# First state-space layer: kernel K directly behind the projection; expert block 0 in another order of steps

## What is computed

```
# state-space part, four layers i
z = layernorm_channels(h); K = 2 * Re(sum_n C[h,n] * exp(dtA[h,n] * l))
y = causal_convolution(z, K) + z * D_skip;  out = W @ gelu(y) + b
h = h + out[:H] * sigmoid(out[H:])
# experts: 12 experts, three routers (top 3 of 12, softmax over the three), 64-wide addresses
x_addr = x @ P_w.T;  dw1, dw2, dw3 = route(x_addr @ U1.T), route(x_addr @ U2.T), route(x_addr @ U3.T)
h = sum_e dw1[:, e] * (x @ W1[e].T);  h = gelu(h)
y = sum_e dw2[:, e] * (h @ W2[e].T) + dw3 @ b2
```

## Time and profile before

| | |
|---|---|
| median of 3 runs | 1193.77 us |
| profiled execution | 1192.28 us, of which the span on the core 1190.2 us |
| PE busy | 1002.9 us (84% of the span) |
| DVE, ACT, POOL busy | 761.6, 530.1, 446.3 us |
| chain that ended last, by engine | PE 57%, DVE 17%, POOL 13%, ACT 6%, issue 4% |
| mean granted TensorE clock | 0.907 of full speed |

### The profile page before, as it was taken

One profiled execution on the slowest core, in us unless ns is written; L12 is line 12 of the kernel. 1 busy time (PEld: TensorE's weight loads), 2 busy tenths in 40 slices (PEclk: granted clock), 3 DMA queues, 4 the chain that ended last, 5 costly groups with the idle time before them and its releaser, 6 DMA issues.

```text
span 1190.2 us, 19912 instructions
## 1 busy us (share of the span) xinstructions
PE 1002.9 (84%) x8002; PEld 668.9 (56%) x8002; DVE 761.6 (64%) x1350; ACT 530.1 (45%) x1230; POOL 446.3 (38%) x470
## 2 busy tenths in 40 slices
PE   6976998865469899999997768589798899969987
PEld 4645564744237687887875523245466534556643
DVE  7693584747566664563646687799566549946653
ACT  6746576462245412021110600067687436768632
POOL 7978115142024400000001344369544238944420
PEclk8978888988669899999999788989799999979999
DMA  3306718072437427346502200000121110012201
GB/s 107 72 1 122 142 29 152 16 126 59 163 120 146 79 48 133 68 106 106 95 12 87 85 0 1 0 1 1 37 47 46 53 68 28 1 37 55 51 6 35
DMA packets 60008, 75.57 MB, mean 63 GB/s; under 512 B 37461, under 2 KB 41953, under 8 KB 58189
## 3 DMA queue, kind: packets, MB, share of 16 engines
q1 hardware_dynamic: 59916, 74.31, 28.5%
HBM read 51.82 MB, written 1.51 MB: 45 GB/s over the span
## 4 chain that ended last, share of the span: by engine, by line
PE 57%; DVE 17%; POOL 13%; ACT 6%; issue 4%; DMA 1%; SPq 0%; POOLq 0%; DVEq 0%
PE psum L1553 7%; PE psum L1555 7%; PE psum L1554 7%; POOL rest L1826 3%; POOL rest L1816 3%; PE psum L2062 3%; POOL rest L1822 3%; PE psum L2069 2%; DVE main L1668 2%; PE psum L2078 2%; ACT rest L1760 2%; PE psum L2134 2%; PE psum L2115 2%; PE psum L742 2%; PE psum L2054 1%
## 5 line engine op out<-in xcount | busy, mean ns | idle before, releaser
L1760 ACT ACTIVATE rest<-psum,main 128x128 f32<-128x128 f32 x256 | 113.3, 482 | 11.5 <-POOL main L1837 11.5
L1245 ACT ACTIVATE x_high<-main 128x512 fp32r<-128x512 f32 x48 | 30.4, 633 | 160.4 <-DVE main L1394 160.4
L435 POOL TENSOR_TENSOR kept<-kept 128x8 f32<-128x8 f32 x6 | 3.2, 530 | 244.4 <-DVE kept L396 244.4
L1852 POOL TENSOR_TENSOR rest<-rest,main 128x512 f32<-128x512 f32 x64 | 65.4, 1042 | 42.2 <-DVE main L1922 42.2
L1553 PE MATMUL psum<-hid_high,w_low 128*128 128x512 f32 x192 | 76.6, 399 | 4.2 <-DVE hid_low L1448 3.4
L1553 PE MATMUL psum<-x_high,w_low 128*128 128x512 f32 x192 | 76.6, 399 | 2.4 <-DVE x_low L1399 2.4
L1555 PE MATMUL psum<-x_high,w_high 128*128 128x512 f32 x192 | 75.7, 394 | 0.0
L1554 PE MATMUL psum<-x_low,w_high 128*128 128x512 f32 x192 | 75.7, 394 | 0.0
L1555 PE MATMUL psum<-hid_high,w_high 128*128 128x512 f32 x192 | 75.5, 393 | 0.0
L1554 PE MATMUL psum<-hid_low,w_high 128*128 128x512 f32 x192 | 75.5, 393 | 0.0
L1394 DVE TENSOR_TENSOR main<-kept,rest 128x512 f32<-128x512 f32 x48 | 39.9, 832 | 48.0 <-PE psum L1555 40.3
(11 more groups left out here) (363 smaller groups left out, 2782.1 us busy)
## 6 DMA issues: line engine op xcount, KB each, us to landing
rest<-share_d SPq DMA_DIRECT2D x4, 3072.0 KB, 21.2
main<-main SPq DMA_DIRECT2D x32, 256.0 KB, 6.3
main<-k_pad SPq DMA_DIRECT2D x16, 512.0 KB, 7.9
rest<-share_d SPq DMA_DIRECT2D x4, 2048.0 KB, 20.2
rest<-main SPq DMA_DIRECT2D x32, 256.0 KB, 3.6
main<-w_dram SPq DMA_DIRECT2D x2, 3072.0 KB, 13.6
main<-rest SPq DMA_DIRECT2D x32, 128.0 KB, 2.3
rest<-tables_dram SPq DMA_DIRECT2D x2, 2048.0 KB, 9.5
```

What stands on the lines that cost most here:

```text
L1760: last = A.activation(probs[:, p, 4 * r + m, :], bank[2 * p + r][:, m * P:(m + 1) * P], ACT.Exp, scale=row_scale[:, c, r, m:m + 1], bias=r ...
L1852: nc.gpsimd.tensor_tensor(probs[:, c % 2, four_heads], probs[:, c % 2, four_heads], row_sum[:, c % 2, four_heads].unsqueeze(2).to_broadcas ...
```

## The change

Layer 0 of the state-space part: PE waits for the transposed projection, then computes K of layer 0, and only then the near angles of layer 2 and the far angles of layer 1. ACT copies K's rows ahead of the roundings instead of behind the sines. DVE turns the state before it takes the turns of those two angles.

Expert block 0: routing of the tokens of blocks 2 and 3 moves from ahead of the hidden values to between the output experts 0 to 6, a step per expert, on tiles of its own. These lie in the last four rows of `share1`, so the DMA of block 1's rows 4 to 11 of router 1 waits for the last weights (`moe_weight` 3). The hidden values wait for `moe_weight` 2 instead of 3. Block 1's routing is spread over one step more and ends at expert 8 instead of 7; its transposes stand behind expert 10 instead of 9, those of blocks 2 and 3 behind output 7 instead of 3. The last exponential stands behind the second weights, with a dummy gelu behind it that brings the gelu table back. ACT takes `share(1)` and `share(2)` ahead of a weight part, DVE the three first weight parts ahead of `raw(0, 0)`, and each `low` directly behind its `raw`.

```
@@ s4_dve_layer
                 s4_dve_powers(dve, 1)
-                s4_dve_near_turns(dve, 2)
-                s4_dve_far_turns(dve, 1)
                 dve.wait_ge(sem("s4_phases"), 1)
...
             link(V.tensor_tensor(b_im, b_im, s_b, ALU.subtract))
+            if L == 0:
+                s4_dve_near_turns(dve, 2)
+                s4_dve_far_turns(dve, 1)
@@ s4_pe_layer
             if L == 0:
+                pe.wait_ge(sem("s4_in"), 1)
+                s4_pe_kernel(pe, 0)
                 s4_pe_near_angles(pe, 2)
-                pe.wait_ge(sem("s4_in"), 1)
                 s4_pe_far_angles(pe, 1)
-                s4_pe_kernel(pe, 0)
@@ moe_act
-            for e in range(AHEAD):
-                share(e)
-                high(0, e)
-                w1_part(e + 3)
+            share(0)
+            high(0, 0)
+            share(1)
+            w1_part(3)
+            high(0, 1)
+            share(2)
+            w1_part(4)
+            high(0, 2)
+            w1_part(5)
...
-                if e == 4:
+                if e == 5:
                     moe_act_exp(act, 1)
-                if e == 5:
                     moe_act_out(act, 2)
...
-            moe_act_exp(act, 2)
             moe_act_wT(act, 1)
-            act.wait_ge(sem("moe_weight"), 3)
+            act.wait_ge(sem("moe_weight"), 2)
             hidden(0)
             for e in range(EXPERTS - 6, EXPERTS):
                 w2_part(e)
+            moe_act_exp(act, 2)
+            A.activation(warm[:, 0:1], warm[:, 1:2], ACT.Gelu)
@@ moe_dve
-            w1_small(0)
+            for e in range(ON_DVE):
+                w1_small(e)
             moe_dve_stats(dve, 2)
...
             raw(0, 0)
-            w1_small(1)
+            low(0, 0)
             raw(0, 1)
-            low(0, 0)
-            w1_small(2)
+            low(0, 1)
             raw(0, 2)
-            low(0, 1)
...
-                if b == 0:
-                    others.best()
-                    others.compared()
-                    others.ranked()
-                    others.chosen()
-                    others.weighed()
                 for m in range(HID_CHUNKS):
...
+                    if b == 0:
+                        if e == 0:
+                            others.marked()
+                            others.read()
+                        if e in (1, 2):
+                            others.best(e - 1, 2)
+                        if e == 3:
+                            others.compared()
...
+                        if e == 6:
+                            others.weighed()
@@ moe_pe
-                        if e == 9:
+                        if e == 10:
                             moe_pe_wT(pe, 1, 1)
...
-                    if b == 0 and e == 3:
+                    if b == 0 and e == 7:
                         moe_pe_wT(pe, 2, 2)
@@ sync
+                if b == 1:
+                    sp.wait_ge(sem("moe_weight"), 3)
                 sp.dma_start(share1[:, SPREAD:], rows1[SPREAD:].partition_broadcast(P)).then_inc(sem("moe_share_in1"), 16)
@@ scalar
             s4_act_sines_near(act, 1)
+            s4_act_k_rows(act, 0)
             s4_act_round_near(act, 2)
             s4_act_round_far(act, 1)
             s4_act_sines_near(act, 2)
-            s4_act_k_rows(act, 0)
```

More of the change, by code:

```diff
@@ L277, in program @@
         share1 = keep(EXPERTS, 512)
+        at_late = top[0] - 4 * 512
         share2 = keep(EXPERTS, 512)
@@ L294, in program @@
         addr = [y[0:ADDR, :] for y in (y_acc, y_part[0])]
+        top[0] = at_late
+        logit_late = keep(ROUTED_TILES, ROUTERS * EXPERTS)
+        above_late = keep(ROUTED_TILES, ROUTERS * EXPERTS)
+        equal_late = keep(ROUTED_TILES, ROUTERS * EXPERTS)
+        ranks_late = keep(ROUTED_TILES, ROUTERS * EXPERTS)
+        fresh_late = keep(ROUTED_TILES, ROUTERS * EXPERTS)
+        top8_late = keep(ROUTED_TILES * ROUTERS, 8)
+        room_late = keep(ROUTED_TILES * ROUTERS)
+        total_late = keep(ROUTED_TILES * ROUTERS)
+        assert top[0] <= at_late + 4 * 512
         weight = spare[:, 0:TILES * ROUTERS * EXPERTS].rearrange("p (c e) -> p c e", c=TILES)
@@ L1340, in __init__, with marked, read, best @@
                     self.wide = [P, self.groups, EXPERTS]
-                    self.logit, self.above, self.equal, self.ranks, self.fresh = (t[:, 0:tiles] for t in (logit, above, equal, ranks, fresh))
-                    self.top8, self.room, self.total = (t[:, 0:self.groups] for t in (top8, room, total))
+                    if n < 2:
+                        self.logit, self.above, self.equal, self.ranks, self.fresh = (t[:, 0:tiles] for t in (logit, above, equal, ranks, fresh))
+                        self.top8, self.room, self.total = (t[:, 0:self.groups] for t in (top8, room, total))
+                    else:
+                        self.logit, self.above, self.equal, self.ranks, self.fresh = logit_late, above_late, equal_late, ranks_late, fresh_late
+                        self.top8, self.room, self.total = top8_late, room_late, total_late
                     self.weight = weight[:, first:first + tiles]
                     self.tiles = tiles
-                def best(self):
+                def marked(self):
+                    link(V.memset(self.fresh, 1.0))
+                    V.memset(g3(self.fresh)[:, :, 0:1], 0.0)
+                def read(self):
                     dve.wait_ge(sem("moe_route_ps"), ROUTED[f"logit{self.n}"])
                     link(V.tensor_copy(self.logit, bank[(4, 5, 7)[self.n]][:, 0:36 * self.tiles].rearrange("p (c e) -> p c e", e=36)))
-                    for k in range(self.groups):
+                def best(self, part=0, parts=1):
+                    size = self.groups // parts
+                    for k in range(size * part, size * (part + 1)):
                         last = V.max(self.top8[:, k, :], g3(self.logit)[:, k, :])
@@ L1404, in moe_dve @@
             first, second, others = (Routing(n) for n in range(3))
+            first.read()
             first.best()
@@ L1427, in moe_dve @@
                         if e == 3:
-                            second.best()
+                            second.read()
+                            second.best(0, 2)
                         if e == 4:
+                            second.best(1, 2)
+                        if e == 5:
                             second.compared()
-                        if e == 5:
+                        if e == 6:
                             second.ranked()
-                        if e == 6:
+                        if e == 7:
                             second.chosen()
-                        if e == 7:
+                        if e == 8:
                             second.weighed()
@@ L1462, in moe_dve @@
                         chain.mark(V.tensor_tensor(y_acc, y_acc, part, ALU.add))
+                    if b == 0:
[6 more added lines that the diff above has]
+                            others.compared()
+                        if e == 4:
+                            others.ranked()
+                        if e == 5:
+                            others.chosen()
+                        if e == 6:
+                            others.weighed()
                     if more and e >= EXPERTS - AHEAD - 1 and e < EXPERTS - 1:
```

## The result

The changed kernel takes 1184.18 us (median of 6 runs, 1183.48 to 1187.75) against 1193.94 us (1193.28 to 1197.93) before: 9.8 us less, a ratio of 0.9912 with a 95% interval of 0.9899 to 0.9925. Run again on another chip, it took 1179.87 us against 1193.90 (ratio 0.989, 0.9858 to 0.9922). The forecast was 1180.9 us, 12.9 us less. The profiled execution took 1183.74 us, its span 1181.9 us; TensorE's mean granted clock was 0.909 (0.907 before), PE busy 85%.

The account below looks back on a forecast made before the run. It took PE's waits as the bound: 12.09 us for `sel` in layer 0, gaps of 1.84 and 3.39 us in expert block 0. Terms 6.9 + 1.8 + 5.2 - 1.0 = 12.9 us gave 1180.9 us, range 1173 to 1188.

Parts of the forecast that it names:

- Layer 0, minus 6.9: Layer 0 reordered with K first: its outputs start at 104.2 instead of 111.15, between minus 1.5 and minus 11 us.
- the first rival: PE's clock stays up in layer 0, exponents at 1.00: layer 0 gives 11 us, total 1176.8; 18 in 100.
- The second: Clock stays low in layer 0's K, or turning delays near turns over one `decay`: layer 0 gives 1.5, total 1186.3; 12 in 100.
- the lock of DVE and POOL: Layer 0: SBUF operations of DVE and POOL pass one at a time, so turning waits for `decay`, 1.8 us more.
- Start of the experts, minus 1.8: Expert block 0, start: `low` is ready earlier, so PE's 1.84 us gap goes; between 0 and minus 3.5 us.
- Middle, minus 5.2: Expert block 0, between halves: PE's 3.39 us gap goes, plus 1.8 us from the clock; between minus 3 and minus 5.5.
- outputs, plus 1.0: Expert block 0, outputs: the moved routing chain just fits DVE's gaps, costing 1 us, between 0 and 3.
- The third rival: Experts' gain is given back, DVE ending the output phase: experts give 2 us, total 1184.9; 12 in 100.
- the slow case: Slower than before: block 1's rows of the router land late and PE waits 21 us, total 1204; 3 in 100.

Follow-up runs that it names:

- e1: The kernel before with only the layer 0 part (order on PE, ACT and DVE), experts as before: 1186.08 us, ratio 0.9937.
- e4: The changed kernel with four added, unused 128-row matmuls on PE between layer 0's far angles and the exponents: 1180.39 us, ratio 0.9885.
- e6: The changed kernel with DVE's near and far turns back ahead of turning the state in layer 0: 1182.90 us, ratio 0.9904.
- e3: The changed kernel with hT of block 2 ahead of the exponential of block 1's routing on ACT: 1180.73 us, ratio 0.9887.
- e8: The changed kernel with DVE's near turns between the fourth and fifth turning operation in layer 0: 1180.01 us, ratio 0.9897.
- e9: The changed kernel with block 0's first half as before; only the routing of blocks 2 and 3 keeps its new place: 1178.12 us, ratio 0.9869.
- e10: The changed kernel with hT of block 2 ahead of the exponential and near turns between the fourth and fifth turning operation: 1174.28 us, ratio 0.9846.
- e11: e10 with four of ten groups of layer 1's transposes on PE between near and far angles and ahead of the exponents: 1176.29 us, ratio 0.9858.

## Why the prediction was right or wrong

**Layer 0, minus 6.9.** Right: 6.7 in e1, 5.9 and 7.0 in the traces of the whole change, 6.9 between the means of all traces with the new and the old order. Its steps came as written: K from 60.91, 9.0 us long, and `sel` at 82.8, in my 83 to 85. The near turns start at 79.08, when DVE is through, and release the exponents at 81.42, where I had 82.1. The exponents took 7.19 us at 0.50 (7.1), which rules out the first rival; e4 has them at 1.00. The second did not come either: K took 9.0 us, and the turning lost 1.7 us to `decay`, once. For the lock of DVE and POOL (Trainium skill, "SBUF — State Buffer", "Who interferes with whom") the trace agrees: L646 took 2.92 us beside `decay` and 1.21 us without it. Not seen ahead: the powers of layer 2 (L561) end at 100.8, 3.1 us before the outputs, and are a bound of their own: in e6, where they end later, the outputs wait for them. POOL's coefficient operations are 19, not 20, which changes nothing in the sum.

**Start of the experts, minus 1.8.** Wrong: plus 0.7 in the trace, outside the range of 0 to minus 3.5, and minus 0.2 in the mean of seven traces. The gap did go. The step that failed is "`moe_act_exp(1)` now stands ahead of hT of block 2, for which PE waits: up to 0.4 us back". I priced only the exponential's own length. It had stood ahead of hT before, too; what was new is that it and the DVE step that it needs came next to hT. What counts is its wait, here 1.85 us for DVE, which was late through a DMA that did not move up and through POOL beside it, and then the clock. The four kernels with hT first put the order's cost at about 2.2 us in stage C; without it the term would have been minus 1.6 to minus 2.8 (50.26 to 49.00 against 51.84). That the rows' late load is the root was followed back in the trace; no run issued it earlier.

**Middle, minus 5.2, and outputs, plus 1.0.** Right: together minus 4.2, measured minus 4.55 in stage D, the same within 0.1 us in all kernels with the move. The hidden products follow L1630 after 1.02 us instead of 4.48, at 1.00, which is 3.46 of it. The rest, 1.1 us, is the clock's gain less what the outputs cost; the two were not measured apart. The outputs cost one wait of 0.67 us that the trace shows. The third rival, DVE ending the phase, did not come, nor did the slow case: the rows were issued at 419.08 and landed at 433.2, 3.4 us before `raw` took them (I had 3). That `raw` started 10.6 us earlier than before, not 13.

**The sum.** The stages give 5.9 (7.0) less 0.7 and plus 4.55: 9.8 and 10.9 us of the predicted 12.9. The span fell by 8.3 us only, since the untouched stages B and E were 2.8 us longer in the trace after and the start 1.3 us shorter. The two medians, 9.8 and 14.0 us less, differ by less than the untouched stage E alone does between traces.

## What to carry to other kernels

Price a step that moves ahead of another on an engine by the wait that it brings along, not by its length, and follow what it waits for back to its DMA. Where compute is pulled ahead, look for the loads that stay where they were. When an idle time on the bounding engine goes, ask which other chains end just under it: with the near turns as the bound, `sel` was ready 5.7 us before PE took it, the state's DMA 5.1 us and the powers 3.1 us before the outputs.

## What the hardware showed that I had not expected

The scatter between executions of one kernel has its place in TensorE's clock. Stages B and E, the same work in all, ranged from 234.75 to 240.96 us and from 710.13 to 718.03 us. Stage E falls into two groups over the fourteen traces. In five (e3, e6, e8, e9, e10) it took 710.1 to 712.1 us, at a mean granted clock of 0.943 to 0.949 and with PE busy for 617 to 619 us; in the other nine 715.7 to 718.0 us, at 0.933 to 0.940 and with PE busy for 623 to 627 us. The matmuls are the same. One stretch of stage E, the second 72 us behind the end of block 3's first half, in the changed kernel and then in e3:

```profile
670.50:742.50 72.00, 56.40 (x112) 0.88 0.00 0
```

```profile
671.20:743.20 72.00, 54.83 (x120) 0.95 0.00 0
```

The near angles, directly behind K, took 5.25 us in the first trace of the changed kernel and 3.69 us in the second, by where the clock fell from 1.00 to 0.50; the exponents then took 7.19 us in every trace with the new order on PE but that of e4. And what a stretch of 128-row work did for the clock differed: 5.8 us of it brought the clock to 1.00 (e4), and two stretches of 1.9 us with 32-row products between them did not (e11).
